# One group in sixteen takes seven gathered tiles and one picked tile, and the layer-two loops are four bodies long

## The reference, cut to what matters

```python
h = jnp.maximum(_layernorm(x), 0.0)
x = x + relu(segment_sum(edge_weight * (h @ W + b)[src], dst) / (segment_sum(edge_weight, dst) + 1e-6))
h = jnp.maximum(_layernorm(x), 0.0)
messages = gelu(concatenate([h[src], edge_attr]) @ W_msg + b_msg)
x = x + gelu(((1 + eps) * h + segment_sum(messages, dst)) @ W_upd + b_upd)
```

## Time and profile before

| | |
|---|---|
| median of three runs | 2618.65 us |
| the profiled execution | 2620.69 us, its span 2618.9 us |
| PE busy | 2437.3 us, 93% of the span |
| POOL busy | 1791.4 us, 68% |
| DVE busy | 2012.4 us, 77% |
| granted PE clock over the span | 0.987 |

### The profile page before, as it was taken

The page is one execution under the profiler, slowest core; times in us unless marked ns, Lnnn a source line. Parts: engine busy times, 40 slices in busy tenths (PEclk is TensorE's granted clock), DMA queues, the critical chain, the costliest instruction groups (busy, mean ns, idle before and its releaser), DMA issues.

```text
span 2618.9 us, 70760 instructions
## 1 busy us (share of the span) xinstructions
PE 2437.3 (93%) x21749; PEld 2273.1 (87%) x21750; DVE 2012.4 (77%) x4216; ACT 1560.6 (60%) x5144; POOL 1791.4 (68%) x1879
## 2 busy tenths in 40 slices
PE   1588899999888888899999999999999999999998
PEld 1477799999888888899999999999999999999998
DVE  7888887766888886777777777777777777777774
ACT  2466666665666664566555656665656566556653
POOL 3377765677777773477777777777777777777771
PEclk9999999999999998899999999999999999999997
DMA  6111111111111110344444444445454544445451
GB/s 117 38 26 27 25 24 21 25 26 26 26 25 24 25 25 22 86 122 119 120 119 121 118 122 118 122 118 125 116 121 120 121 119 119 119 120 120 118 121 37
DMA packets 472280, 213.80 MB, mean 82 GB/s; under 512 B 264668, under 2 KB 441656, under 8 KB 472196
## 3 DMA queue, kind: packets, MB, share of 16 engines
q1 hardware_dynamic: 412548, 151.55, 22.1%
q0 software_dynamic: 59648, 61.20, 12.8%
HBM read 207.09 MB, written 5.51 MB: 81 GB/s over the span
## 4 chain that ended last, share of the span: by engine, by line
PE 58%; DVE 0%; ACT 0%; issue 0%; DVEq 0%
PE ps L930 43%; PE ps L1135 7%; PE ps L1000 4%; PE ps L1124 3%; PE ps L1082 1%; PE ps L1029 0%; DVE rows L1473 0%; DVE parts L1231 0%; DVE sel L1469 0%; DVE room L1675 0%; ACT h_sb L860 0%; DVE h_sb L1706 0%; DVE h_sb L1711 0%; ACT h_sb L878 0%; DVE tick L1510 0%
## 5 line engine op out<-in xcount | busy, mean ns | idle before, releaser
L639 POOL DMA_INDIRECT rows<-p_table,idx x1176 | 1109.8, 944 | 390.0 <-issue 342.8
L930 PE MATMUL ps<-parts,pick_all 128*128 128x448 f32 x5488 | 1162.0, 369 | 2.6 <-DVE parts L1231 2.6
L930 PEld LDWEIGHTS ps<-parts,pick_all 128*128 128x128 f32 x5488 | 1019.4, 189 | 77.7 <-issue 2.9
L639 POOL DMA_INDIRECT rows<-h_table,idx x688 | 665.3, 967 | 324.3 <-issue 200.9
L940 PE MATMUL ps<-hot_c,hot_p 128*128 128x150 f32 (+4 forms) x2336 | 435.0, 313 | 64.9 <-issue 37.1
L1469 DVE TENSOR_TENSOR sel<-ps,mask 128x896 f32<-128x896 f32 x196 | 214.0, 1092 | 307.0 <-PE ps L930 298.3
L940 PEld LDWEIGHTS ps<-hot_c,hot_p 128*128 128x128 f32 x2336 | 371.7, 192 | 85.7 <-issue 63.8
L731 ACT COPY adj<-ps 128x500 f32<-128x500 f32 (+4 forms) x880 | 349.9, 448 | 149.5 <-PE ps L940 136.9
L1452 DVE TENSOR_SCALAR pick_all<-src_all,node_f 128x1792 fp32r<-128x1792 int16 x196 | 406.5, 2074 | 27.4 <-issue 24.7
L1406 DVE TENSOR_SCALAR hot_p<-iota_p,scal 128x128 f32<-128x128 f32 (+2 forms) x880 | 301.1, 342 | 76.5 <-PE ps L940 56.0
L1473 DVE TENSOR_REDUCE rows<-sel 128x128 f32<-128x896 f32 x196 | 342.7, 1749 | 6.7
(11 more groups left out here) (182 smaller groups left out, 2345.0 us busy)
## 6 DMA issues: line engine op xcount, KB each, us to landing
src_all<-keys SPq DMA_DIRECT2D x196, 448.0 KB
ea<-in_edge_attr_dram SPq DMA_DIRECT2D x196, 256.0 KB
rows<-p_table,idx POOLq DMA_INDIRECT x1176
rows<-h_table,idx POOLq DMA_INDIRECT x688
x_sb<-in_x_dram SPq DMA_DIRECT2D x6, 224.0 KB, 4.3
h_table<-h_sb SPq DMA_DIRECT2D x6, 224.0 KB
p_table<-h_sb SPq DMA_DIRECT2D x6, 224.0 KB
out_dram<-h_sb SPq DMA_DIRECT2D x6, 224.0 KB
```

What stands on the lines that cost most here:

```text
L639: nc.gpsimd.indirect_dma_start(out=rows[:, s, j, 0:D], out_offset=None, in_=table[:, :], in_offset=bass.IndirectOffsetOnAxis(ap=idx[:, s, ...
L930: last = nc.tensor.matmul(to, hot[:, k, t * P:(t + 1) * P], parts[:, part, k, :, :].rearrange("p a d -> p (a d)"), start=(k == 0 and part ...
```

## The change

Layer two's loops on PE, DVE and POOL now hold four bodies (`LOOP = 4`, phases 0 to 3), and run 12 rounds; the last body stays behind them. In phase 3 the group in the last slot gathers seven tiles and picks one. The loops of ACT and SP stay one body long, and so do the one-hot matrix (made for two tiles, always) and the load of source numbers.

```diff
+    LOOP = 4
+        def one_pick(phase, slot):
+            return phase == LOOP - 1 and slot == SLOTS - 1
...
-                        for j in tiles:
+                        for j in range(tiles.start, tiles.stop + one_pick(phase, s)):
...
-                    with pool.Fori(BODIES + 1, 2 * BODIES) as turn:
-                        gathers(turn, range(J0))
+                    with pool.Fori(0, (BODIES - 1) // LOOP) as i:
+                        for phase in range(LOOP):
+                            gathers(i * LOOP + (BODIES + 1 + phase), range(J0), phase)
...
-                for t in range(PICKS):
+                for t in range(one_pick(phase, q), PICKS):
...
-            with pe.Fori(0, BODIES - 1) as b:
-                second(b, False)
-            second(BODIES - 1, True)
+            with pe.Fori(0, (BODIES - 1) // LOOP) as i:
+                for phase in range(LOOP):
+                    second(i * LOOP + phase, phase, False)
+            second(BODIES - 1, 0, True)
...
+                own = slice(int(one_pick(phase, q)), PICKS)
...
+                landed = 16 * GATHERED + (b + (s + shift) // SLOTS + 1) * (16 * J0)
+                if slot == SLOTS - 1:
+                    landed = landed + (i + one_pick(phase, slot)) * 16
+                dve.wait_ge(s_gat[slot], landed)
```

More of the change, by code:

```diff
@@ L184, in two_layer_gnn @@
     J0 = J - PICKS
+    LOOP = 4
+    assert (BODIES - 1) % LOOP == 0
     GATHERED = ZONES[-1].gathered(BODIES)
@@ L628, in _, with gathers @@
                 pool.wait_ge(s_tabw[layer], (UNITS + 1) * 16)
-                def gathers(turn, tiles):
+                def gathers(turn, tiles, phase=0):
                     for s in range(SLOTS):
@@ L916, in _, with picks @@
                 turn(w_raw, half, psR[half])
-            def picks(b, q):
+            def picks(b, q, phase=0):
                 hot = pick_all[:, q % 2, :].rearrange("p (k e) -> p k e", k=KA)
@@ L1142, in _, with second @@
             edge_product(0, 0, 0)
-            def second(b, last_body):
+            def second(b, phase, last_body):
                 for s in range(SLOTS):
@@ L1147, in second @@
                         edge_transpose(b, s, 1)
-                        picks(b, s + 1)
+                        picks(b, s + 1, phase)
                     last_group = last_body and s == SLOTS - 1
@@ L1459, in next_pick, with picked_rows @@
                 make_pick(b, q)
-            def picked_rows(b, q):
+            def picked_rows(b, q, phase=0):
                 g = b * SLOTS + q
@@ L1467, in picked_rows @@
                 dve.wait_ge(s_prow, g + 1)
[L1468 to L1471, removed]
+                own = slice(int(one_pick(phase, q)), PICKS)
+                n = PICKS - own.start
+                of = mask[:, bass.ds(g, 1), own, :].rearrange("p g t a -> p (g t) a")
+                nc.vector.tensor_tensor(sel[:, own, :, :],
+                                        ps[:, bank + own.start:bank + PICKS, 0:NA * D].rearrange(
+                                            "p t (a d) -> p t a d", d=D),
+                                        of.unsqueeze(3).to_broadcast([P, n, NA, D]), ALU.mult).then_inc(s_sel, 1)
                 dve.wait_ge(s_sel, g + 1)
-                nc.vector.tensor_reduce(rows[:, q % SLOTS, J0:J, 0:D],
-                                        sel[:, :, :, :].rearrange("p t a d -> p t d a"),
+                nc.vector.tensor_reduce(rows[:, q % SLOTS, J0 + own.start:J, 0:D],
+                                        sel[:, own, :, :].rearrange("p t a d -> p t d a"),
                                         AX.X, ALU.add).then_inc(s_prow, 1)
@@ L1664, in _, with message_sum @@
             dve.wait_ge(s_cleared, 1)
-            def message_sum(b, s, shift):
+            def message_sum(b, s, shift, phase=0, i=0):
                 slot = (s + shift) % SLOTS
@@ L1670, in message_sum @@
                 dve.wait_ge(s_em, g + 1)
-                dve.wait_ge(s_gat[slot], 16 * GATHERED
-                            + (b + (s + shift) // SLOTS + 1) * (16 * J0))
+                landed = 16 * GATHERED + (b + (s + shift) // SLOTS + 1) * (16 * J0)
+                if slot == SLOTS - 1:
+                    landed = landed + (i + one_pick(phase, slot)) * 16
+                dve.wait_ge(s_gat[slot], landed)
                 dve.wait_ge(s_prow, g + 2)
@@ L1680, in _, with second @@
             message_sum(0, 0, 0)
-            def second(b, last_body):
+            def second(b, phase, last_body, i):
                 for s in range(SLOTS):
@@ L1692, in second @@
                     if not (last_body and s == SLOTS - 1):
-                        picked_rows(b, s + 1)
-                        message_sum(b, s, 1)
+                        picked_rows(b, s + 1, phase)
+                        message_sum(b, s, 1, phase, i)
                     if s % 2:
@@ L1697, in second @@
                         sums(1, b, s, P, odd, more)
-            with dve.Fori(0, BODIES - 1) as b:
-                second(b, False)
-            second(BODIES - 1, True)
+            with dve.Fori(0, (BODIES - 1) // LOOP) as i:
+                for phase in range(LOOP):
+                    second(i * LOOP + phase, phase, False, i)
+            second(BODIES - 1, 0, True, (BODIES - 1) // LOOP)
             for u in range(UNITS + 1):
```

## The result

| kernel | median us | lowest to highest | runs |
|---|---|---|---|
| before | 2616.89 | 2602.18 to 2619.41 | 4 |
| changed | 2656.39 | 2655.16 to 2657.52 | 4 |

The changed kernel takes 1.0168 of the time before, with a 95% interval of 1.0135 to 1.0200: it is slower, by 44 us at the middle of the interval.

The account below looks back on a forecast made before the run. PE was taken to bound layer two, 30.70 us a body, POOL close behind. Pick savings of -34.0 us plus 58.3 us of back-edge stalls gave +24.3 on 2618.65, so 2643 us; range 2616 to 2670, the forecast's own 2634 to 2666.

Parts of the forecast that it names:

- The stall at the back edge: PE's four-body loop, 10.3 packets, is not kept; each of 11 back edges costs 5.3 us, 58.3 us in all.
- Its idle time: PE idles 3.6 us at each taken back edge of layer two's loop, bounds 2.8 and 4.0 us.
- Its lower clock: Behind each PE stall the clock halves for 3.4 us, losing 1.7 us; at best 0, at worst 3.4.
- both rows 12 cases: Lower-clock stretches on PE behind idle times: 3.4 us long, losing 1.7 us, or 6.8 us long, losing 3.4.
- The rival that the clock holds: PE stalls at its back edges but the clock stays full: +5.6 us, 2624 us; chance 0.12.
- The pick products: One-tile group on PE: 14 products instead of 28 save 2.835 us a round, 34.0 us over 12 rounds.
- the one on DVE's mask and sum: DVE handles one tile instead of two, 1.4 us less a round; said to be worth and cost nothing.
- The added gathers: POOL gets 12 more gathers of 1.248 us, 15.0 us, hidden while PE's round is over POOL's 121.1 us.
- DVE's own back edge: DVE's edge may take 4.0 us, its matrix 3.5 us later; PE's stall covers it, otherwise 1.3 us late.
- The kept-code rival: PE keeps four bodies' code and POOL decides: last message sum at 2565.3, -19.3 us, 2599 us; chance 0.15.

Follow-up runs that it names:

- the same work in 5.1 packets: The changed kernel with three equal bodies of each round made passes of an inner loop on PE and DVE: 2602.39 us, ratio 0.9947.
- the run with the moved end: The changed kernel with 50 unused products on PE ahead of layer two's loop, without the back-edge hint: 2642.04 us, ratio 1.0102.
- the hint and the moved end: The changed kernel with 50 unused products ahead of PE's layer-two loop and a back-edge hint on that loop: 2588.80 us, ratio 0.9922.

## Why the prediction was right, step by step

*The stall at the back edge* was the step on which the forecast turned, and it is shown. Ten packets are not kept (134 loaded, where none were), a jump to code that isn't there stops PE, and the same work in 5.1 packets, or with the jump announced in time, is faster than before.

*Its idle time* was sized at 3.6 us with bounds of 2.8 and 4.0; it measured 4.2, outside. The branch at L1038 was the right model for one packet fetched in the open (3.3 us once the loop's end was moved). Not foreseen was the second packet, which I take for the code behind the loop, fetched at the same time. That this comes from the loop's end standing just behind a packet's border is borne out by the run with the moved end, where the second packet was gone from the edge.

*Its lower clock* was sized at 1.7 us from a 3.4 us stretch and measured 1.6 to 1.7 for ten edges, and 2.2 for the one whose stretch is 6.8 us, since PE was busy in 4.49 us of it: both rows 12 cases came. The rival that the clock holds fell.

*The pick products* were sized at 2.83 us a round and gave 2.48. The step that failed is the one on DVE's mask and sum, which was said to be worth nothing and to cost nothing: it looked at DVE's wait ahead of a mask, not at PE's wait for the next one-hot matrix. With a shorter group PE has less work to cover DVE's 6.75 us, and loses 0.35 us of it twelve times, 4.1 us.

Idle time, clock and this wait together make +36 for the +24.3 of the sum: 11 x 0.6 = 7 too little for idle time, 0.5 for the longer stretch, 4 for DVE. That the time still lies between 2634 and 2666 us owes something to luck: the idle time passed its bound, but the clock's term stayed far below its dearest value of 3.4 us. And the end of the program, which no term of the sum held, ran at the lower clock in both profiled executions; at the full clock it is 12 us shorter (last section).

*The added gathers* stayed hidden as forecast. POOL waits longer for its indices, since PE's round is longer than POOL's 121.1 us; from 1090 to 2640 us:

```profile
POOL rows L645 <- ACT idx L677: 53.4, 63, 4.2
```

Single waits reach 4.2 us, where they reached 0.8.

*DVE's own back edge* reloads too, with idle times of up to 3.4 us:

```profile
DVE pick_all L1460 <- issue: 37.2, 21, 3.4
```

PE's stall covers them, as forecast, since PE waits for no matrix at the edge; without the stall it costs PE 1.2 us a round (13.0 in all), for which 1.3 was worked out.

*The kept-code rival* did not happen, but its working did when the stall was taken away: it put the last message sum at 2565.3 with POOL as the bound, and with the hint and the moved end it is at 2562.52 with POOL as the bound.

## What to carry to other kernels

Before unrolling a loop further, count its code in instruction packets from the trace (executed instructions between two loads) and look whether the queue lists packets inside the loop: as long as it lists none, the back edge is free, and once it lists them each turn costs the fetch of the loop's start and, on PE, the clock behind it, unless the branch is announced early enough. An inner loop over the equal bodies gives the same work without that price. A saving on one engine shifts the wait to whatever the saved time used to cover, so ask for each shortened piece which other engine worked beside it.

## What the runs showed of the hardware that was not expected

How much it helps to announce a branch depends on where the loop's end lies in its packet: the branch takes 2.95 us where it stands now, which I take for just behind a border, and 0.46 us a hundred instructions further, with about as many packets loaded (125 and 130 from 1130 to 2550 us). Other places were not tried.

The end of the program behind layer two comes in two lengths, by the granted clock. From the last message sum to the end of the span it is 34.3 us in the kernel before and 34.5 in the changed one, but 22.5 with the hint and the moved end. In the stretch that follows the sum, for the changed kernel and for that one (columns as in the earlier trace rows):

```profile
2624.50:2655.70 31.20, 26.25 (x133) 25.63 (x133) 8.18 (x14) 4.04 (x7) 0.00 (x0) 0.50 0.21 52
```
```profile
2562.50:2583.50 21.00, 15.26 (x167) 14.73 (x165) 9.46 (x19) 4.67 (x8) 0.00 (x0) 1.00 0.32 77
```

The instructions are the same; only the clock differs, and with it 12 us. Of the ten profiled kernels four ended at 0.50 and six at 1.00, and neither the change nor the length of layer two decides which. The runs of the kernel before go from 2600 to 2623 us, about as wide; whether these two ends make that spread is not shown, as only profiled runs tell where the clock was low. The others tell its mean over the span, and that fits: of 41 runs, the seven with a mean of 0.991 or more took 2600 to 2609 us, the nine with 0.981 or less 2615 to 2623. For a change in layer two the last message sum is the better measure, and what sets the clock of the end is open.
